# A selective-scan block with two feed-forward layers on one core: the split of a layer norm's last step between GpSimdE and VectorE, two and two tiles or three and one

## The chip, the cores and the metric

One core of a Trainium2 chip. The time is device microseconds (us) of one execution; of several executions the median counts. Engines: TensorE (PE in rows; PEld its weight loads), VectorE (DVE), ScalarE (ACT), GpSimdE (POOL), SyncE (SP), which issues most DMAs.

## What is computed

Two sequences of 2048 tokens of width 256, float32. Every `_layernorm` below has no scale and no offset.

```python
x = x + 0.5 * ffn(_layernorm(x), W1, b1, W2, b2)      # 8 groups of 512 tokens, own weights each
x = x + ssm(_layernorm(x), ...)                        # state-space layer, 512 channels x 16 states
x = x + 0.5 * ffn(_layernorm(x), W1, b1, W2, b2)

def ffn(x): h1 = x @ W1.T + b1 ; return h1 @ W2.T + b2  # linear twice
def step(h, inp):                                       # in ssm, over the tokens
    dt_t, u_t = inp
    h = h * exp(dt_t * A) + dt_t * Bm * u_t             # per channel and state
    return h, sum over states of h * Cm
out = (ys * silu(z)) @ Wo.T + bo + x * Dv.mean()        # z, u, dt from x @ Wi.T + bi
```

## The kernel before, in words

The 4096 tokens go through in four iterations of 1024 (`NIT`, `TOK`). In each there are four blocks of 128 channels, 16 blocks `k` in all, and of each block 16 **scans**: one VectorE instruction (line 1209) runs the recurrence over 1024 tokens for 128 pairs of channel and state, in place in one of 8 buffers of `G` (`NG`). Blocks 0 and 15 are cut in halves of 512 tokens, so there are 288 scans.

Beside each scan there is fixed work: ScalarE makes its factor (`exp`, line 1089) in the same `G` buffer. After four scans TensorE sums over states into `Y` (`red`, line 1376) and so sets free the four buffers that ScalarE fills for the scans 8 places on. Everything else (projections, feed-forward layers, norms, output projection, merging W1 and W2 into one matrix) is cut in chains of small steps.

What sets the order: `schedule` walks the scans and after each lets every waiting chain give out its next step. `PLAN`, `DTS` and `PROJ` say after which scan a chain starts, `rest_for(WAIT)` keeps a step back by some scans. Each engine has the same list and executes its own part strictly in that order; semaphores tie the engines together. So the order is fixed when the kernel is built, whatever the durations are.

A **norm** is the chain `norm(c)`, `c` from 0 to 23, six for each iteration: of 512 tokens, which are four tiles of 128 tokens x 256. Its steps: `sq` on ScalarE (line 910), then `var` (823), `rstd` (832, a power), `sr` (837) and `off` (842) on tiny 128x4 operands, then the normalising itself, `xn = v * rstd + off`, one instruction of 128x256 a tile. Norms 0 to 3 and 23 are `early(c)`: VectorE does nearly all, and nothing is changed in them. Of the other 19 all small steps run on GpSimdE, and the last step is split: `norm` on GpSimdE (line 849) does tiles 2 and 3, `vnorm` on VectorE (line 1186) does tiles 0 and 1, placed among the scans at least six scans behind `norm` where `rest_for(WAIT)` applies. I number these 19 norms in the order of time, norm 1 to norm 19.

Both parts must be done before TensorE transposes the result (`xt`, line 1280); ScalarE copies it out (`xtc`, line 936). GpSimdE's queue also holds `skip` (lines 860 to 863: eight 128x256 tiles in each iteration, in place in `X`) and `msv` (line 869: two 128x256 tiles of a merged weight matrix, for which TensorE's line 1260 waits).

Of the kernel before, what the change touches and what calls it, by code (L numbers as in the profile page):

```python
# [100 lines left out]
def early(c):  # L101

    return c < 4 or c == 23


def made(stage, c):

    return ("v" if early(c) else "") + stage


def normed(c):

    return ("vnorm",) if early(c) else ("norm", "vnorm")
# [513 lines left out]
def build(nc, x, w, wit, wdt, wot, bo, cols, masks, out):  # L627
# [3 lines left out]
    with ctx:  # L631
# [67 lines left out]
        def tiles(pr):  # L699

            return slice(2 * pr[0], 2 * pr[0] + 2) if pr else slice(0, 4)

        def tokens(c):
            it, ph, hf = c // 6, c % 6 // 2, c % 2
            return it, ph, hf, X[:, (2 * it + hf) % NX, :, :], LV[:, c % 6, :, :], XN[:, place[c] % 2, :, :]
# [100 lines left out]
        @block.gpsimd  # L806
        def _(eng):
            e = Engine(eng, count, sems)

            def do(stage, *a):  # L810
                if stage == "calm":
                    eng.memset(ZS[:, 0, 0:512], 0.0).then_inc(sems["calm"])
                elif stage == "ones":
                    eng.memset(ONES[:, :], 1.0).then_inc(sems["ones"])
                elif stage == "half":
                    eng.memset(HIGH[:, :], TOP)
                    eng.memset(ZERO[:, :], 0.0)
                    eng.memset(HALF[:, :], -0.5).then_inc(sems["half"])
                elif stage == "var":
                    c, = a  # L820
                    lv = tokens(c)[4]
                    e.wait_ge("sq", c)
                    eng.tensor_scalar(lv[:, 1, :], lv[:, 1, :], 2.0 ** -24, EPS, ALU.mult, ALU.add).then_inc(sems["var"])  # L823
                elif stage == "rstd":
                    c, *pr = a
                    lv, ts = tokens(c)[4], tiles(pr)
                    e.wait_ge(made("var", c), *a)
                    e.wait_ge("half")
                    if c >= 6:
                        for part in normed(c - 6):  # L830
                            e.wait_ge(part, c - 6)
                    eng.tensor_tensor(lv[:, 3, ts], lv[:, 1, ts], HALF[:, ts], ALU.pow).then_inc(sems["rstd"])  # L832
                elif stage == "sr":
                    c, = a
                    lv = tokens(c)[4]
                    e.wait_ge("rstd", c)
                    eng.tensor_tensor(lv[:, 2, :], lv[:, 0, :], lv[:, 3, :], ALU.mult).then_inc(sems["sr"])
                elif stage == "off":
                    c, = a
                    lv = tokens(c)[4]  # L840
                    e.wait_ge("sr", c)
                    eng.tensor_scalar(lv[:, 4, :], lv[:, 2, :], -1.0 / 256, float(c % 6 // 2 != 1), ALU.mult, ALU.add
                                      ).then_inc(sems["off"])
                elif stage == "norm":
                    c, = a
                    _, _, _, v, lv, xn = tokens(c)
                    e.wait_ge("off", c)
                    for i in (2, 3):
                        ins = eng.tensor_scalar(xn[:, i, :], v[:, i, :], lv[:, 3, i:i + 1], lv[:, 4, i:i + 1],  # L849
                                                ALU.mult, ALU.add)  # L850
                    ins.then_inc(sems["norm"])
                elif stage == "skip":
                    c, i = a
                    _, _, _, v, lv, _ = tokens(c)
                    e.wait_ge("dmu")
                    e.wait_ge(made("sr", c), c)
                    for part in normed(c):
                        e.wait_ge(part, c)
                    if i == 0:
                        eng.tensor_scalar(lv[:, 5, :], lv[:, 3, :], DM[:, 0:1], 1.0, ALU.mult, ALU.add)  # L860
                        eng.tensor_scalar(lv[:, 6, :], lv[:, 2, :], DM[:, 1:2], -1.0, ALU.mult, ALU.mult).then_inc(sems["skips"])
                        eng.wait_ge(sems["skips"], (count.value["skip", a] + 3) // 4)
                    eng.tensor_scalar(v[:, i, :], v[:, i, :], lv[:, 5, i:i + 1], lv[:, 6, i:i + 1],  # L863
                                      ALU.mult, ALU.add).then_inc(sems["skip"])
                elif stage == "msv":
                    g, = a
                    e.wait_ge("mv", g)
                    for i in range(2):
                        ins = eng.tensor_scalar(MS[:, i, 0:256], MS[:, i, 0:256], 1.0, MV[:, i:i + 1], ALU.mult, ALU.add)  # L869
                    ins.then_inc(sems["msv"])  # L870

            schedule(do)
# [222 lines left out]
        def _(eng):  # L1095
            e = Engine(eng, count, sems)

            def do(stage, *a):
# [61 lines left out]
                elif stage == "vvar":  # L1160
                    c, *pr = a
                    lv, ts = tokens(c)[4], tiles(pr)
                    e.wait_ge("sq", *a)
                    eng.tensor_scalar(lv[:, 1, ts], lv[:, 1, ts], 2.0 ** -24, EPS, ALU.mult, ALU.add).then_inc(sems["vvar"])  # L1164
                elif stage == "vsum":
                    c, = a
                    it, _, hf, v, lv, _ = tokens(c)
                    e.wait_ge("x", 2 * it + hf)
                    eng.tensor_reduce(lv[:, 0, :], v, AX.X, ALU.add).then_inc(sems["vsum"])  # L1169
                elif stage == "vsr":  # L1170
                    c, *pr = a
                    lv, ts = tokens(c)[4], tiles(pr)
                    e.wait_ge("rstd", *a)
                    eng.tensor_tensor(lv[:, 2, ts], lv[:, 0, ts], lv[:, 3, ts], ALU.mult).then_inc(sems["vsr"])
                elif stage == "voff":
                    c, *pr = a
                    lv, ts = tokens(c)[4], tiles(pr)
                    e.wait_ge("vsr", *a)
                    eng.tensor_scalar(lv[:, 4, ts], lv[:, 2, ts], -1.0 / 256, float(c % 6 // 2 != 1), ALU.mult, ALU.add
                                      ).then_inc(sems["voff"])  # L1180
                elif stage == "vnorm":
                    c, *pr = a
                    _, _, _, v, lv, xn = tokens(c)
                    e.wait_ge(made("off", c), *a)
                    for i in range(4 if early(c) else 2)[tiles(pr)]:
                        ins = eng.tensor_scalar(xn[:, i, :], v[:, i, :], lv[:, 3, i:i + 1], lv[:, 4, i:i + 1],
                                                ALU.mult, ALU.add)
                    ins.then_inc(sems["vnorm"])
                elif stage == "w":
                    k, p = a  # L1190
                    t0, t1 = span(k, p)
                    for hf in halves(k, p):
                        e.wait_ge("u", k, hf)
                    e.wait_ge("dt", k, p)
                    d = DW[:, 1, t0:t1]
                    eng.tensor_tensor(d, d, DW[:, 0, t0:t1], ALU.mult).then_inc(sems["w"])
                elif stage == "scan":
                    i, = a
                    k, p, m, q = parts(i)
                    t0, t1 = window(k, p)  # L1200
                    idx = states(i)
                    e.wait_ge("repw", k, q, fed(k, p))
                    e.wait_ge("exp", i)
                    goes_on = p > 0 or k // 4 % 2 > 0
                    if goes_on:
                        ko, po = (k, p - 1) if p else scanned(k - 4)
                        e.wait_ge("save", AT[ko, po, 4 * m])
                    g = G[:, i % NG, t0:t1]
                    eng.tensor_tensor_scan(g, g, RV[:, (4 * k + q) % NR, t0:t1], STT[:, idx:idx + 1] if goes_on else 0.0,  # L1209
                                           ALU.mult, ALU.add).then_inc(sems["scan"])  # L1210
                elif stage == "yz":
                    k, p = a
                    t0, t1 = window(k, p)
                    e.wait_ge("red", AT[k, p, 12])
                    for hf in sides(k, p):
                        e.wait_ge("z", k, hf)
                    z = ZS[:, k % NZ, t0:t1]
                    eng.tensor_tensor(z, z, Y[:, t0:t1], ALU.mult).then_inc(sems["yz"])  # L1218
# [239 lines left out]
```

## Time and profile before

| | us |
|---|---|
| median of 3 runs | 768.38 (767.89 to 770.54) |
| the profiled execution | 768.11 |
| its span in the trace | 766.3 |
| VectorE busy | 669.7 (87%) |
| TensorE matmuls busy | 640.7 (84%) |
| ScalarE busy | 603.2 (79%) |
| GpSimdE busy | 301.7 (39%) |

Of 38 `norm` instructions on GpSimdE one takes 2.2 us on average, of 58 on VectorE 0.45 us. A VectorE instruction overlaps the one behind it by 0.08 us in the rows, so its cost in a queue is its duration less that. Scans of 1024 tokens last 2.25 to 2.5 us.

### The profile page before, as it was taken

Reading aid. Unit: us, or ns where it says so; the run is one execution under the profiler, and the core shown is the slowest. Engines: PE = TensorE matmul, PEld = TensorE weight load, DVE = VectorE, ACT = ScalarE, POOL = GpSimd, SP = SyncE. Lnnn points to the kernel's source line nnn. Section 1 sums busy time; section 2 is a strip of 40 time slices with the busy share of each in tenths; the row PEclk is TensorE's granted clock in tenths of the full one; section 3 lists DMA queues with packets and bytes.
Section 4 is the critical chain, followed back from the end, with each engine's and each line's share of the span. In section 5 each row is a group of like instructions: output and inputs, shape, how many; then the busy total and the mean of one; then the engine's idle time right before and its main releaser. Section 6 shows DMA issues by size and latency. Waiting matters only on the chain. (4 is left out here: it accounts for less than half of the span.)

```text
span 766.3 us, 8284 instructions
## 1 busy us (share of the span) xinstructions
PE 640.7 (84%) x2912; PEld 331.8 (43%) x2912; DVE 669.7 (87%) x463; ACT 603.2 (79%) x1066; POOL 301.7 (39%) x189
## 2 busy tenths in 40 slices
PE   7967786889886999979898999967867997874958
PEld 5642333364342466445244574622322654241727
DVE  2436948779999999999999999999999999999791
ACT  2478896779798989998788989898889787946454
POOL 0107020034344598569920767066940060600030
PEclk9997898989997899999999999996988999896979
DMA  8330476350838070421567150705161504205001
GB/s 299 139 137 28 160 219 184 125 178 28 313 117 313 1 246 2 172 103 60 215 198 269 50 198 13 262 1 219 28 216 59 216 31 176 99 28 219 2 0 56
DMA packets 40026, 103.08 MB, mean 135 GB/s; under 512 B 4080, under 2 KB 13040, under 8 KB 39984
## 3 DMA queue, kind: packets, MB, share of 16 engines
q1 hardware_dynamic: 37424, 94.40, 33.7%
q10 hardware_dynamic: 2560, 8.14, 4.5%
q8 instruction: 23, 0.38, 0.2%
q14 instruction: 19, 0.16, 0.1%
HBM read 23.08 MB, written 4.19 MB: 36 GB/s over the span
## 5 line engine op out<-in xcount | busy, mean ns | idle before, releaser
L1089 ACT ACTIVATE G<-RD,COL 128x1024 f32<-128x1024 f32 (+1 forms) x288 | 280.0, 1043 | 62.0 <-PE Y L1376 55.6
L1209 DVE TENSOR_TENSOR_SCAN G<-G,STT,RV 128x1024 f32<-128x1024 f32 (+1 forms) x160 | 312.5, 2015 | 6.4 <-ACT G L1089 6.4
L1209 DVE TENSOR_TENSOR_SCAN G<-G,RV 128x1024 f32<-128x1024 f32 (+1 forms) x128 | 268.9, 2157 | 13.4 <-ACT G L1089 13.4
L1376 PE MATMUL Y<-G,RW 128*32 128x512 f32 x1024 | 143.7, 678 | 62.2 <-DVE G L1209 58.9
L823 POOL TENSOR_SCALAR LV<-LV 128x4 f32<-128x4 f32 x19 | 16.2, 854 | 298.0 <-ACT XN L910 297.7
L1376 PEld LDWEIGHTS Y<-G,RW 128*32 128x32 f32 x1024 | 27.8, 116 | 143.2 <-DVE G L1209 81.5
L849 POOL TENSOR_SCALAR XN<-X,LV 128x256 f32<-128x256 f32 x38 | 83.9, 2212 | 2.0
L1343 PE MATMUL MB<-XI,DIAG 128*64 128x512 f32 x248 | 62.8, 644 | 13.0 <-DMA XI<-XI 11.1
L1302 PE MATMUL MB<-MT,XF 128*128 128x256 f32 x240 | 62.3, 406 | 13.3 <-ACT MT L952 7.6
L832 POOL TENSOR_TENSOR LV<-LV,HALF 128x4 f32<-128x4 f32 (+1 forms) x25 | 45.9, 1837 | 63.5 <-DVE LV L1164 61.9
L1321 PE MATMUL MB<-XT,WI 128*128 128x512 f32 x128 | 64.1, 629 | 3.7 <-ACT XT L936 3.7
L863 POOL TENSOR_SCALAR X<-X,LV 128x256 f32<-128x256 f32 x32 | 63.9, 2007 | 0.8
L1354 PE MATMUL MB<-XT,WI 128*128 128x512 f32 x128 | 59.6, 614 | 3.4 <-ACT XF L936 2.6
L1400 PE MATMUL MB<-WO,ZS 128*128 128x256 f32 x256 | 61.8, 379 | 0.0
L869 POOL TENSOR_SCALAR MS<-MS,MV 128x256 f32<-128x256 f32 x12 | 27.2, 2271 | 85.2 <-DVE MV L1143 85.2
L1302 PEld LDWEIGHTS MB<-MT,XF 128*128 128x128 f32 x240 | 48.3, 203 | 22.8 <-ACT XF L936 9.3
L1400 PEld LDWEIGHTS MB<-WO,ZS 128*128 128x128 f32 x256 | 48.8, 191 | 6.7
L1250 PE MATMUL MB<-W 128*128 128x257 f32 x192 | 47.9, 395 | 2.6 <-DMA W<-in_w 2.5
L910 ACT ACTIVATE XN<-X,LV 128x256 f32<-128x256 f32 x96 | 47.5, 499 | 1.6 <-DVE LV L1169 1.1
L1009 ACT ACTIVATE XI<-MB,COL 64x512 f32<-64x512 f32 x64 | 43.3, 676 | 4.0 <-PE MB L1321 3.5
L1156 DVE SCALAR_TENSOR_TENSOR DW<-MB,COL,DW 128x512 f32<-128x512 f32 x32 | 22.2, 732 | 25.7 <-ACT DW L1067 25.7
L1250 PEld LDWEIGHTS MB<-W 128*128 128x128 f32 x192 | 35.2, 192 | 20.8 <-issue 9.7
(93 smaller groups left out, 774.5 us busy)
## 6 DMA issues: line engine op xcount, KB each, us to landing
RD<-DW SPq DMA_DIRECT2D x60, 512.0 KB, 3.8
RV<-DW SPq DMA_DIRECT2D x60, 512.0 KB, 4.7
W<-in_w SPq DMA_DIRECT2D x48, 256.5 KB, 3.7
XI<-XI ACTq DMA_DIRECT2D x30, 256.5 KB, 5.0
X<-in_x SPq DMA_DIRECT2D x8, 512.0 KB, 5.6
out<-X SPq DMA_DIRECT2D x7, 512.0 KB, 3.2
G<-in_w SPq DMA_DIRECT2D x4, 513.0 KB, 7.8
RV<-in_w SPq DMA_DIRECT2D x4, 513.0 KB, 12.3
```

The costliest lines, as they stand in the source:

```text
L849: ins = eng.tensor_scalar(xn[:, i, :], v[:, i, :], lv[:, 3, i:i + 1], lv[:, 4, i:i + 1], ALU.mult, ALU.add)
L863: eng.tensor_scalar(v[:, i, :], v[:, i, :], lv[:, 5, i:i + 1], lv[:, 6, i:i + 1], ALU.mult, ALU.add).then_inc(sems["skip"])
L910: ins = eng.activation(xn[:, i, :], v[:, i, :], ACT.Square, bias=lv[:, 0, i:i + 1], scale=-256.0, accum_out=lv[:, 1, i:i + 1])
L1089: eng.activation(G[:, i % NG, t0:t1], RD[:, q, t0:t1], ACT.Exp, scale=NAC[:, states(i):states(i) + 1]).then_inc(sems["exp"])
L1209: eng.tensor_tensor_scan(g, g, RV[:, (4 * k + q) % NR, t0:t1], STT[:, idx:idx + 1] if goes_on else 0.0, ALU.mult, ALU.add).then_inc(sems[" ...
L1250: ins = eng.matmul(bank("merge", g, i)[:, 0:257], v[:, 257 + 128 * i:385 + 128 * i], v[:, 0:257], start=(c == 0), stop=(c == 7))
L1302: ins = eng.matmul(o, xf[:, j, 128 * t:128 * t + 128], MT[:, g % NX, j, :], start=False, stop=(i == 1 and j == 1))
L1321: ins = eng.matmul(bank("xim", k, hf), WI[:, j, 128 * ct:128 * ct + 128], XT[:, j, 512 * hf:512 * hf + 512], start=(j == 0), stop=(j == 1))
L1343: ins = eng.matmul(bank("um", k, hf)[64 * g:64 * g + 64, :], DIAG[:, 4 * ct + 2 * g + t, :], XI[:, g, 512 * hf + 2 * t:512 * hf + 2 * t + ...
L1354: ins = eng.matmul(bank("zm", k, hf), WI[:, j, 512 + 128 * ct:640 + 128 * ct], XT[:, j, 512 * hf:512 * hf + 512], start=(j == 0), stop=(j ...
L1376: ins = eng.matmul(Y[32 * q:32 * q + 32, 512 * h:512 * h + 512], RW[:, states(i + o), :], G[:, (i + o) % NG, 512 * h:512 * h + 512], start ...
L1400: ins = eng.matmul(o, ZS[:, (4 * it + ct) % NZ, 128 * (2 * pr + i):128 * (2 * pr + i) + 128], WO[:, ct, :], start=False, stop=(i == 1 and ...
```

## The change

Each of the 19 norms that are not early gives one more tile to GpSimdE: tiles 1, 2 and 3 there, tile 0 on VectorE. Early norms keep all their four on VectorE; norm 23, in two pairs, keeps them too.

```diff
                 elif stage == "norm":
                     e.wait_ge("off", c)
-                    for i in (2, 3):
+                    for i in (1, 2, 3):
                         ins = eng.tensor_scalar(xn[:, i, :], v[:, i, :], lv[:, 3, i:i + 1], lv[:, 4, i:i + 1],
                                                 ALU.mult, ALU.add)
...
                 elif stage == "vnorm":
                     e.wait_ge(made("off", c), *a)
-                    for i in range(4 if early(c) else 2)[tiles(pr)]:
+                    for i in range(4 if early(c) else 1)[tiles(pr)]:
```

No instruction changes its place against the others; TensorE, ScalarE and SyncE have the same lists. On VectorE, from norm 5 to norm 9 (`L1186` are the norms, `L1209` the scans, 280 to 336 us in the trace), a part of the difference:

```order
-L1186 TENSOR_SCALAR XN<-X,LV 128x256 x2
+L1186 TENSOR_SCALAR XN<-X,LV 128x256
 L1209 SCALAR_TENSOR_TENSOR G<-G,STT,RV 128x1024 x6
-L1186 TENSOR_SCALAR XN<-X,LV 128x256 x2
+L1186 TENSOR_SCALAR XN<-X,LV 128x256
 L1209 SCALAR_TENSOR_TENSOR G<-G,STT,RV 128x1024 x4
-L1186 TENSOR_SCALAR XN<-X,LV 128x256 x2
+L1186 TENSOR_SCALAR XN<-X,LV 128x256
```

These are norms 7, 8 and 9: one tile instead of two stands between the scans, at the same places.

On GpSimdE at the same norms, where one norm's steps stand right behind the other's:

```order
-L849 TENSOR_SCALAR XN<-X,LV 128x256 x2
+L849 TENSOR_SCALAR XN<-X,LV 128x256 x3
 L823 TENSOR_SCALAR LV<-LV 128x4
 L832 TENSOR_TENSOR LV<-LV,HALF 128x4
 L837 TENSOR_TENSOR LV<-LV 128x4
 L842 TENSOR_SCALAR LV<-LV 128x4
-L849 TENSOR_SCALAR XN<-X,LV 128x256 x2
+L849 TENSOR_SCALAR XN<-X,LV 128x256 x3
```

The third tile stands ahead of the next norm's four small steps, and so ahead of the `off` for which that norm's VectorE tile waits.

At norm 11 GpSimdE has a merged weight matrix behind the norm (`MS`, line 869), in the changed kernel:

```order
L837 TENSOR_TENSOR LV<-LV 128x4
L842 TENSOR_SCALAR LV<-LV 128x4
L849 TENSOR_SCALAR XN<-X,LV 128x256 x3
L869 TENSOR_SCALAR MS<-MS,MV 128x256 x2
L823 TENSOR_SCALAR LV<-LV 128x4
```

Three tiles instead of two stand ahead of the two of `MS`.

## Rows read from the trace of the kernel before

**Rows 1.** The page, busy us of each engine.
```profile
PE 640.7 (84%) x2912; PEld 331.8 (43%) x2912; DVE 669.7 (87%) x463; ACT 603.2 (79%) x1066; POOL 301.7 (39%) x189
```
**Rows 2.** Stretches: start:end, length, busy us (instructions) by engine, clock, DMA.
```profile
166.00:300.00 134.00, 119.83 (x570) 61.16 (x567) 131.71 (x79) 120.33 (x204) 79.91 (x43) 0.95 0.42 146
300.00:440.00 140.00, 124.78 (x584) 60.82 (x583) 138.38 (x80) 123.08 (x202) 83.53 (x43) 0.98 0.41 144
440.00:582.00 142.00, 117.59 (x562) 57.52 (x562) 140.24 (x81) 123.92 (x217) 79.56 (x43) 0.90 0.39 136
```
**Rows 3.** Waits: engine, tile, line, releaser; total us, times, longest.
```profile
DVE G L1209 <- ACT G L1089: 19.8, 9, 5.5
...
PE MB L1260 <- POOL MS L869: 7.4, 3, 4.3
...
DVE XN L1186 <- POOL LV L842: 0.7, 2, 0.4
```
**Rows 4.** Groups by form: the two lines that the change touches.
```profile
L1186 DVE TENSOR_SCALAR XN<-X,LV 128x256 f32<-128x256 f32 x58 | 23.4, 450 | 0.9 <-POOL LV L842 0.7
...
L849 POOL TENSOR_SCALAR XN<-X,LV 128x256 f32<-128x256 f32 x38 | 83.9, 2212 | 2.0
```
**Rows 5.** Timeline of VectorE: start, us to the last end, line, count.
```profile
296.97 0.72 DVE L1186 TENSOR_SCALAR XN<-X,LV 128x256 f32<-128x256 f32 x2
...
466.83 9.03 DVE L1209 TENSOR_TENSOR_SCAN G<-G,RV 128x1024 f32<-128x1024 f32 x4
...
479.91 21.90 DVE L1209 TENSOR_TENSOR_SCAN G<-G,RV 128x1024 f32<-128x1024 f32 x10
```
**Rows 6.** Timeline of GpSimdE: single norm tiles at three places.
```profile
102.23 0.56 POOL L849 TENSOR_SCALAR XN<-X,LV 128x256 f32<-128x256 f32 x1
...
471.52 4.55 POOL L849 TENSOR_SCALAR XN<-X,LV 128x256 f32<-128x256 f32 x1
...
512.15 2.51 POOL L849 TENSOR_SCALAR XN<-X,LV 128x256 f32<-128x256 f32 x1
```
**Rows 7.** Timeline at norm 5: GpSimdE, then TensorE there and around.
```profile
277.07 5.33 POOL L849 TENSOR_SCALAR XN<-X,LV 128x256 f32<-128x256 f32 x2
282.49 2.04 POOL L823 TENSOR_SCALAR LV<-LV 128x4 f32<-128x4 f32 x1
...
248.57 3.64 PE L1376 MATMUL Y<-G,RW 128*32 128x512 f32 x16 [0.95 <-DVE G L1209]
...
286.32 1.04 PE L1280 MATMUL MB<-COL,XN 128*128 128x128 f32 x8
...
310.21 1.93 PE L1376 MATMUL Y<-G,RW 128*32 128x512 f32 x16 [0.19 <-DVE G L1209]
```
**Rows 8.** Timeline at norm 9 and behind it: GpSimdE, VectorE, ScalarE.
```profile
328.67 2.04 POOL L823 TENSOR_SCALAR LV<-LV 128x4 f32<-128x4 f32 x1
...
335.52 0.91 DVE L1186 TENSOR_SCALAR XN<-X,LV 128x256 f32<-128x256 f32 x2 [0.32 <-POOL LV L842]
...
354.57 4.60 DVE L1209 TENSOR_TENSOR_SCAN G<-G,STT,RV 128x1024 f32<-128x1024 f32 x2 [1.09 <-ACT G L1089]
...
353.38 4.27 ACT L1089 ACTIVATE G<-RD,COL 128x1024 f32<-128x1024 f32 x4
```
**Rows 9.** Timeline at norm 11: the merged weights on GpSimdE, their transpose.
```profile
436.09 4.85 POOL L869 TENSOR_SCALAR MS<-MS,MV 128x256 f32<-128x256 f32 x2
...
443.60 0.60 PE L1260 MATMUL MB<-COL,MS 128*128 128x128 f32 x4
```
**Rows 10.** Timeline at norms 14 and 15: GpSimdE's small steps, VectorE.
```profile
514.75 0.20 POOL L823 TENSOR_SCALAR LV<-LV 128x4 f32<-128x4 f32 x1
515.03 3.10 POOL L832 TENSOR_TENSOR LV<-LV,HALF 128x4 f32<-128x4 f32 x1
...
518.83 0.91 DVE L1186 TENSOR_SCALAR XN<-X,LV 128x256 f32<-128x256 f32 x2 [0.38 <-POOL LV L842]
...
425.37 1.02 POOL L832 TENSOR_TENSOR LV<-LV,HALF 128x4 f32<-128x4 f32 x1
```
**Rows 11.** Timeline at norm 19, the last: GpSimdE and TensorE.
```profile
741.65 3.11 POOL L849 TENSOR_SCALAR XN<-X,LV 128x256 f32<-128x256 f32 x2
...
743.97 1.93 PE L1376 MATMUL Y<-G,RW 128*32 128x512 f32 x8 [2.77 <-DVE G L1209]
```

## The prediction

> **What bounds the kernel now.** I read the page first: VectorE is the busiest engine, 669.7 of 766.3 us, GpSimdE has the most room [rows 1]. A share over the whole span proves little, so the stretches come next. From 166 to 582 us VectorE works 131.71 of 134, 138.38 of 140 and 140.24 of 142 us (the rows overlap by 0.08 us an instruction, so true idle time is a little more); TensorE and ScalarE are at 83 to 90% there [rows 2]. Read alone, this says that a microsecond off VectorE is a microsecond off the kernel. The waits say otherwise: VectorE still waits nine times, 19.8 us in all, for ScalarE's factors [rows 3], and in the saturated part one of these waits is at 354.57 us (1.09 us) [rows 8]. Such a wait pins the time to another engine: what VectorE had saved on the way there it would only wait longer. Last, who waits for GpSimdE: TensorE for the merged weights, 7.4 us in three waits, and VectorE for `off` in two short ones, 0.7 us [rows 3]. GpSimdE has room on average, but some of its results are taken the moment they are ready.
>
> **What is removed.** 19 instructions on VectorE. Two in a row with no neighbour on GpSimdE take 0.72 us [rows 5]; less the overlap, 0.32 each. Their mean is 450 ns [rows 4], so 0.37 with the dearer ones. Gross: 19 x 0.32 = 6.1 us, to 19 x 0.37 = 7.0 us.
>
> **What is added.** 19 instructions on GpSimdE. Where no scan runs one takes 0.56 us; beside scans 2.51 or 4.55 us [rows 6], mean 2.2 [rows 4]. The pattern in the rows: a tile issued inside a scan with another scan behind ends 0.2 us behind the *second* scan's end (4.55 us, at 471.52); one with something short behind the scan ends behind the first (2.51 us, at 512.15). A third tile is issued just where the second ended, most often 0.2 us into a scan, so I take 4.6 us where two scans follow, 2.5 where one does, and 0.56 as the lower end.
>
> The Trainium skill, "SBUF — State Buffer", section "Who interferes with whom", says that a VectorE instruction with two SBUF inputs and a GpSimdE instruction that reads SBUF exclude each other, and that the later one "fully blocks" until the first finishes. The 4.55 us row does not agree: it outlasts the first scan by a whole one.
>
> It also costs VectorE. Ten scans without a big GpSimdE instruction take 21.90 us, 2.18 each; four with one that ends among them take 9.03 instead of 8.80 us [rows 5], so 0.23 us at most for one; other places with several give about 0.1, and the tile that ends beside another instruction may cost nothing. I take 0.13, range 0 to 0.23. Net on VectorE 0.32 - 0.13 = 0.2 us a norm (0.1 to 0.37).
>
> **Which norms' gains reach the end.** Norms 1 and 2 lie ahead of 166 us, where VectorE waits for others. TensorE waits for a scan at 248.57 us and then not again before 310.21 [rows 7]; the wait at 354.57 hangs on ScalarE's exponentials from 353.38 us [rows 8], whose chain leads back over projections on TensorE to that unbroken run. So norms 5 to 9 gain nothing by this count, nor 11 and 12 in the like run of TensorE from 414 to 475 us, nor 18 and 19. Left are norms 3, 4, 10, 13, 14 and 16, and at most norm 17: 6 x 0.2 = **-1.2 us**.
>
> **Where the third tile is late.** Four places.
>
> *Norm 5.* Its two tiles end at 277.07 + 5.33 = 282.40, TensorE takes them at 286.32 [rows 7]: slack 3.9 us. A third tile beside scans adds 4.6: TensorE waits 0.7 us. With one tile gone on VectorE the next scan stands earlier, so the second tile, too, may find two scans instead of one: 2 us more, 2.7. TensorE has no gap before 310, so this passes on. Range 0 to 2.7, I take the middle of 0.7 and 2.7 and round down: **+1.6**.
>
> *Norms 8 and 9.* GpSimdE starts norm 9 at 328.67, right behind norm 8, and VectorE already waits 0.32 us for its `off` at 335.52 [rows 8]. A later start moves VectorE's wait. GpSimdE had 12 us of room ahead of norm 8, but norms 5, 6 and 7 stand back to back and bring 2.5 to 4.6 us each with them. By the steps I get a start of norm 9 some 6 us later, of which most is given back, because once VectorE stands still the four small steps take 0.2 + 1.0 + 0.2 + 0.2 us (1.02 for the power [rows 10]) in place of 8: VectorE waits 2.3 us at norm 9 and 0.3 at norm 8. Against this stand the gains of norms 5 to 9 (1.0), the 1.09 us that it waits at 354.57 anyway, and norm 5's 1.6 by which ScalarE is later there: **0**, range 0 to +2.6.
>
> *Norm 11.* The merged weights end at 436.09 + 4.85 = 440.94, TensorE takes them at 443.60 [rows 9]: slack 2.66. The third tile adds 2.5 to 4.6: 0 to 1.9 us of wait in an unbroken run of TensorE. **+1.0**.
>
> *Norm 15.* The second tile of norm 14 is issued at 512.15 and ends at 514.66 [rows 6]; norm 15's steps start at 514.75 and VectorE waits for them at 518.83, 0.38 us [rows 10]. The third tile (2.6 us) moves the start to 517.3. A tensor_tensor of two SBUF inputs runs to 518.1, then the steps take 0.2 + 1.0 + 0.3 + 0.2: the tile starts at 519.85 instead of 518.83. **+1.0**, range 0 to 2.6. Its own three tiles, two beside scans, end some 7 us later than now, but TensorE then stands idle until about 528.8 us, and so this hides; its cover is gone if they take over 9 us.
>
> At norm 19 the tiles end at 741.65 + 3.11 = 744.76. TensorE is busy on the sums from 743.97 to 745.90 [rows 11]; a third at 0.58 (the neighbour is a VectorE tile, not a scan) ends at 745.3: nothing. The other norms have 5 us of room or more behind them.
>
> **Sum.** -1.2 + 1.6 + 0 + 1.0 + 1.0 = +2.4 us. On the profiled execution, 768.11 us (span 766.3 and 1.8 around it), 770.5; it stood 0.3 us under the median of 768.38, so 770.8 us.
>
> **Rivals.**
>
> *The saving wins.* The pinned stretches are not pinned, since the order lets gains through over ScalarE's slack, and the third tile fits in the rooms. Then 16 norms from the third to the eighteenth give 0.2 each, -3.2 us, less one wait of about 0.4: 765.6. For it: VectorE is at 98% for over 400 us [rows 2]. Against: the wait at 354.57, and that GpSimdE's lateness has to be under 2.66 us at norm 11 and 3.9 at norm 5. It decides where third tiles average below 2.5 us.
>
> *One scan is waited for, not two.* A third tile costs 2.5 us everywhere. Norm 5's slack of 3.9 and norm 11's of 2.66 hold, only norm 15's wait stays: -1.2 + 1.0 = -0.2, so 768.2. For it: the mean of 2.2 us [rows 4]. Against: the 4.55 us row stands exactly where third tiles will.
>
> This is what the skill's rule, named above, would make of it: blocked to the end of the running instruction and no further.
>
> *The backlog passes on.* Norms that stand back to back hand their delay on and nothing gives it back: 2.7 at norm 5, 2.6 at norms 8 and 9 (VectorE behind TensorE's delay, not beside it), 1.9 and 2.6 at norms 11 and 15, less 1.2: +8.6, of which two parts overlap; I take +6.5, 774.9. For it: VectorE waits at `off` of norms 9 and 15 already. Against: the small steps are fast once VectorE stands.
>
> *It does not do what it says:* excluded, since the lists of both engines show one instruction less and one more at each of the 19 places.
>
> **Chances.** Forecast 0.45 (769 to 773.5, half over and half under the bound), one scan 0.20 (0.14 within, 0.06 faster), saving wins 0.15, backlog 0.20. What a measurement can tell from no change is 0.3%, here 2.3 us: under 766.1 or over 770.7. Faster 0.06 + 0.15 = 0.21; same 0.20 + 0.14 = 0.34; slower 0.25 + 0.20 = 0.45. The range takes in the savings case and most of the backlog: 765.4 to 775.5.
>
> **What the profile after will show.** Line 849 x57 at a mean over 2.6 us, GpSimdE busy some 50 us more, line 1186 x39. VectorE's waits for line 842 (0.7 us now) grow to 3 us or more, at norms 8, 9 and 15, and TensorE's waits for line 849, absent now, appear at norm 5. If these waits stay under 1 us the forecast is wrong towards faster; if `L1209 <- L1089` grows by the whole saving, the pinning is right. Scans beside third tiles longer by over 0.3 us each would make it wrong towards slower.

## The result

| | before | after |
|---|---|---|
| median | 768.13 us | 781.61 us (776.49 to 785.23, 4 executions) |
| ratio, 95% interval | | 1.0169 (1.0122 to 1.0216) |
| the profiled execution | 768.11 | 785.23 |
| its span | 766.3 | 783.4 |

The changed kernel is slower by 1.7%, some 13 us. The forecast was 770.8 us with a range up to 775.5: the sign was right, the size far too small. Ratios here and below leave out executions that lie over 1.5% above the fastest of their kernel: two of the ten of n11_only, whose median without them is 771.2 us, and one of the kernel before, at 1583 us.

The page of the kernel after, busy us of each engine, answers [rows 1]:

```profile
PE 651.5 (83%) x2912; PEld 336.6 (43%) x2912; DVE 664.8 (85%) x444; ACT 604.0 (77%) x1066; POOL 322.4 (41%) x208
```

VectorE is 4.9 us lighter, GpSimdE 20.7 us heavier, as the diff says. TensorE, whose instructions are the same, is busy for 10.8 us more. That is the first hint of where to look, and no more than a hint: roomy15 below is 0.5% slower than before and has 648.1 us there.

The groups by form of the kernel after, the two lines of the change ([rows 4]):

```profile
L849 POOL TENSOR_SCALAR XN<-X,LV 128x256 f32<-128x256 f32 x57 | 120.0, 2113 | 2.0
...
L1186 DVE TENSOR_SCALAR XN<-X,LV 128x256 f32<-128x256 f32 x39 | 15.5, 428 | 2.7 <-POOL LV L842 2.4
```

The mean of a GpSimdE tile has not grown (2.11 us, 2.21 before). An average says nothing here; what counts is which tiles are the dear ones. The waits of the kernel after (us in total, times, longest), against [rows 3]:

```profile
DVE G L1209 <- ACT G L1089: 27.1, 11, 5.5
...
PE MB L1280 <- issue: 12.6, 2, 9.9
...
PE MB L1260 <- POOL MS L869: 10.5, 3, 4.2
...
DVE XN L1186 <- POOL LV L842: 2.4, 3, 1.8
```

VectorE waits 7.3 us more for ScalarE's factors, which is more than the 4.9 us that it is less busy. TensorE waits 3.1 us more for the merged weights (3.9 at norm 11, where it did not wait before, and less elsewhere), and 12.6 us in two places ahead of the transposes of `XN` (line 1280). "issue" names no releaser, but the first of them ends 0.1 us behind the end of GpSimdE's third tile; here are both queues at norm 5, timelines of GpSimdE and TensorE of the kernel after (start, us to the last end):

```profile
279.98 9.85 POOL L849 TENSOR_SCALAR XN<-X,LV 128x256 f32<-128x256 f32 x3
...
289.94 1.06 PE L1280 MATMUL MB<-COL,XN 128*128 128x128 f32 x8 [2.71 <-issue]
```

279.98 + 9.85 = 289.83, and TensorE goes on at 289.94.

**Where the time is.** The scans are the same 288 instructions in the same order in every kernel, so the starts of the same few scans, read from VectorE's timeline, cut the span into stretches that can be compared. The stretches run from the last four scans ahead of norm 5's VectorE tiles to the wait at 354.57 us, then to the scan at 425.47, over norm 11 to 477.71, to 507.46, over norms 14 to 16 to 577.82 (times of before), and to the last scan. Two of these starts, the kernel before and then after:

```profile
425.47 2.28 DVE L1209 TENSOR_TENSOR_SCAN G<-G,RV 128x1024 f32<-128x1024 f32 x1
...
477.71 2.28 DVE L1209 TENSOR_TENSOR_SCAN G<-G,RV 128x1024 f32<-128x1024 f32 x1
```

```profile
431.86 2.29 DVE L1209 TENSOR_TENSOR_SCAN G<-G,RV 128x1024 f32<-128x1024 f32 x1
...
489.98 2.28 DVE L1209 TENSOR_TENSOR_SCAN G<-G,RV 128x1024 f32<-128x1024 f32 x1
```

So norm 11's stretch has grown from 52.2 to 58.1 us. The same for all stretches and for the kernels of the experiments below (us, worked out from such starts; in bold where three tiles at a tight norm stand in it):

| kernel | first scan of the cut | norm 5 | between | norm 11 | between | norms 14 to 16 | to the last scan |
|---|---|---|---|---|---|---|---|
| before | 270.15 | 84.4 | 70.9 | 52.2 | 29.8 | 70.4 | 164.8 |
| after | 270.81 | **87.6** | 73.5 | **58.1** | 30.1 | **73.2** | 165.7 |
| tight4 | 266.96 | **92.1** | 74.1 | **58.3** | 29.9 | **72.2** | 164.9 |
| roomy15 | 269.61 | 85.6 | 71.1 | 52.1 | 29.9 | 71.7 | 165.9 |
| n5_only | 268.73 | **92.1** | 74.1 | 52.7 | 29.9 | 70.4 | 164.8 |
| n5_again | 268.33 | **91.1** | 72.2 | 52.5 | 29.9 | 70.4 | 165.5 |
| n11_only | 268.70 | 83.5 | 73.8 | **59.0** | 30.1 | 70.4 | 165.2 |
| n15_only | 270.50 | 83.3 | 73.6 | 52.9 | 29.9 | **70.9** | 165.1 |

The kernel after loses 3.2 us at norm 5, 5.9 at norm 11, 2.8 at norms 14 to 16, and 0.3 to 0.9 us in each of the other parts of the span. The 2.6 us "between" norm 5 and norm 11 are not the change's: n15_only and n11_only have the kernel before's code up to there and show 2.7 and 2.9 too. It is the profiled execution of before that is quick there, as the granted clock shows (stretches 369 to 407 us; busy us of PE, PEld, DVE, ACT, POOL, then clock and DMA), before and after:

```profile
369.00:407.00 38.00, 32.72 (x146) 12.99 (x144) 37.83 (x22) 31.66 (x44) 19.71 (x8) 0.99 0.62 206
```

```profile
369.00:407.00 38.00, 33.95 (x136) 13.83 (x128) 35.11 (x21) 29.35 (x38) 20.84 (x9) 0.91 0.54 185
```

Each kernel has one trace, so an entry of the table is good to about 1 us: over norm 5, too, n11_only and n15_only have the code of before, and they take 83.5 and 83.3 us where before took 84.4. Against them the kernel after loses 4.2 us there, not 3.2. The two spans differ by 17.1 us and the medians by 13.5; the profiled execution of the kernel after is itself 3.6 us above its median.

The scans themselves are not what grew: the durations of all 288 add up to 598.4 us before and 599.9 after, and those beside a third tile are mostly 0.10 to 0.14 us longer.

### The profile page after: what moved, and what is told of

It is laid out like the page before. It is cut to its first block, busy times and chain, and to the rows that moved or that the text cites. A ratio compares the mean times of both kernels' runs of the same rounds, so it can differ in the third digit from the quotient of the medians.

```text
span 783.4 us, 8284 instructions
## 1 busy us (share of the span) xinstructions
PE 651.5 (83%) x2912; PEld 336.6 (43%) x2912; DVE 664.8 (85%) x444; ACT 604.0 (77%) x1066; POOL 322.4 (41%) x208
## 4 chain that ended last, share of the span: by engine, by line
PE 47%; ACT 26%; POOL 8%; DVE 7%; DMA 5%; issue 5%; ACTq 1%; SPq 0%; DVEq 0%; POOLq 0%
ACT G L1089 11%; PE Y L1376 9%; DVE G L1209 6%; PE MB L1400 6%; PE MB L1302 6%; POOL XN L849 5%; PE MB L1250 5%; PE MB L1343 5%; PE MB L1354 5%; DMA XI<-XI 3%; ACT XI L1009 3%; PE MB L1321 3%; PE MB L1294 2%; PE MB L1396 2%; ACT XN L910 2%
## 5 line engine op out<-in xcount | busy, mean ns | idle before, releaser
L1209 DVE TENSOR_TENSOR_SCAN G<-G,STT,RV 128x1024 f32<-128x1024 f32 (+1 forms) x160 | 313.2, 2017 | 11.8 <-ACT G L1089 10.7
L1209 DVE TENSOR_TENSOR_SCAN G<-G,RV 128x1024 f32<-128x1024 f32 (+1 forms) x128 | 269.9, 2165 | 16.6 <-ACT G L1089 16.5
L823 POOL TENSOR_SCALAR LV<-LV 128x4 f32<-128x4 f32 x19 | 19.0, 1000 | 296.4 <-ACT XN L910 296.0
L849 POOL TENSOR_SCALAR XN<-X,LV 128x256 f32<-128x256 f32 x57 | 120.0, 2113 | 2.0
L1343 PE MATMUL MB<-XI,DIAG 128*64 128x512 f32 x248 | 66.3, 674 | 10.4 <-DMA XI<-XI 8.6
L1400 PE MATMUL MB<-WO,ZS 128*128 128x256 f32 x256 | 65.1, 394 | 0.0
L863 POOL TENSOR_SCALAR X<-X,LV 128x256 f32<-128x256 f32 x32 | 56.2, 1766 | 0.8
L1400 PEld LDWEIGHTS MB<-WO,ZS 128*128 128x128 f32 x256 | 51.0, 199 | 7.7
L1250 PE MATMUL MB<-W 128*128 128x257 f32 x192 | 49.6, 406 | 1.9 <-DMA W<-in_w 1.9
L1280 PE MATMUL MB<-COL,XN 128*128 128x128 f32 x184 | 28.4, 305 | 20.7 <-issue 12.6
```

The costliest lines, as they stand in the source:

```text
L1250: ins = eng.matmul(bank("merge", g, i)[:, 0:257], v[:, 257 + 128 * i:385 + 128 * i], v[:, 0:257], start=(c == 0), stop=(c == 7))
L1343: ins = eng.matmul(bank("um", k, hf)[64 * g:64 * g + 64, :], DIAG[:, 4 * ct + 2 * g + t, :], XI[:, g, 512 * hf + 2 * t:512 * hf + 2 * t + ...
L1400: ins = eng.matmul(o, ZS[:, (4 * it + ct) % NZ, 128 * (2 * pr + i):128 * (2 * pr + i) + 128], WO[:, ct, :], start=False, stop=(i == 1 and ...
```

## The experiments

Ratios are to the kernel before, run on the same chip between the others, with 95% intervals. Where a kernel has one line more, line 849 is L850, 1209 is L1210 and so on.

### Which norms carry it: tight4 and roomy15

```diff
+THIRD = (12, 18, 20, 11)
...
-                    for i in (2, 3):
+                    for i in ((1, 2, 3) if c in THIRD else (2, 3)):
...
-                    for i in range(4 if early(c) else 2)[tiles(pr)]:
+                    for i in range(4 if early(c) else 1 if c in THIRD else 2)[tiles(pr)]:
```

These are norms 5, 11, 15 and 16 in the order of the program. roomy15 has the other fifteen numbers in `THIRD`.

> The third tile goes to GpSimdE only at norms 5, 11, 15 and 16, the four behind which TensorE waits 2.7, 3.9, 9.9 and 1.9 us in the changed kernel. Lateness theory: these four carry nearly all of the loss, 10 to 14 us slower than before (778 to 782). Contention theory (every third tile lengthens VectorE's scans): 4 of 19 of the loss, 3 us slower (771). Clock theory (TensorE's clock falls after the waits and this is most of the loss): as the first in time, but with TensorE busy 8 us or more above before.

> The other 15 norms give their third tile to GpSimdE, the four stay at two and two. Lateness theory: no place where TensorE waits for GpSimdE beyond what it did before; 0 to 2 us faster than before (766 to 768). Contention theory: 15 of 19 of the loss, 10 us slower (778).

**tight4** 780.08 us, 1.0169 (1.0126 to 1.0213). **roomy15** 771.28 us, 1.0053 (1.0033 to 1.0073). Four of 19 norms cost as much as the whole change. The two parts make 2.2% together, the change 1.7%; the intervals are too wide to call that a difference, but one cost of roomy15 is not there in the kernel after, as the rows below show. And fifteen norms together, each of which frees VectorE of a tile, gain nothing; they lose half a per cent, which neither expectation had (766 to 768 or 778). One of their losses is the wait that the prediction worked out at norms 8 and 9 (2.3 us). GpSimdE, TensorE and VectorE of roomy15:

```profile
322.49 11.88 POOL L850 TENSOR_SCALAR XN<-X,LV 128x256 f32<-128x256 f32 x3
...
334.42 1.97 PE L1281 MATMUL MB<-COL,XN 128*128 128x128 f32 x8 [3.07 <-POOL XN L850]
...
336.34 0.41 DVE L1187 TENSOR_SCALAR XN<-X,LV 128x256 f32<-128x256 f32 x1 [2.18 <-POOL LV L843]
```

Norm 8's three tiles end at 334.37; only then can GpSimdE make norm 9's `off`, for which VectorE waits 2.18 us. In the kernel after the same wait is 0.32 us, as before the change [rows 8].

### One norm at a time: n5_only, n11_only, n15_only

```diff
+THIRD = (12,)
```

and `(18,)` and `(20,)`, the rest as in tight4.

> The third tile goes to GpSimdE at norm 5 alone. Lateness theory: TensorE waits 2.7 to 4.9 us for norm 5 (it did in the two runs with it), the scans behind are 3 us later from about 312 us on, and the kernel is 2 to 5 us slower than before. If the places add up only with the others, less than 2 us.

> The third tile at norm 11 alone, behind which GpSimdE has two tiles of merged weights. The prediction's step gives a TensorE wait of 0 to 1.9 us at line 1260 and 1 us in all. If the runs so far show the size (waits of 3.9 and 4.1 us there, the scans 6.7 us later from 452 to 480 us): 4 to 7 us slower.

> The third tile at norm 15 alone. Lateness theory: TensorE waits 6 to 9 us for it near 540 us, most of it time in which it stood idle before anyway (4.8 us), 1 to 3 us slower. Prediction's step: 1 us.

**n5_only** 777.61 us, 1.0112 (1.0067 to 1.0158). **n11_only** 772.64, 1.0054 (1.0022 to 1.0086). **n15_only** 770.93, 1.0026 (0.9993 to 1.0058). One moved instruction of 128x256 at norm 5 costs about 1% of the kernel, 9.4 us where I had expected 2 to 5 of that run; norm 11 alone is at the lower end of what was expected, and for norm 15 alone the interval takes in no change. The queues, GpSimdE and TensorE of n5_only:

```profile
277.90 11.97 POOL L850 TENSOR_SCALAR XN<-X,LV 128x256 f32<-128x256 f32 x3
...
289.97 1.94 PE L1281 MATMUL MB<-COL,XN 128*128 128x128 f32 x8 [4.90 <-ACT X L988]
...
293.41 2.63 PE L1401 MATMUL MB<-WO,ZS 128*128 128x256 f32 x8
```

The three tiles end at 289.87, TensorE goes on 0.1 us behind; the releaser that the row names had long been done. Then two things are to be seen. TensorE waits 4.90 us, not the 0.7 to 2.7 of the prediction. And its next instructions are slow: eight transposes take 1.94 us, in [rows 7] 1.04; eight matmuls at line 1401 take 2.63, a little further on and at full clock 1.89. The granted clock of those us (stretch of n5_only, columns as above):

```profile
290.00:295.50 5.50, 5.50 (x19) 4.76 (x20) 5.50 (x4) 4.12 (x15) 5.25 (x4) 0.55 0.00 0
```

Taken by single microseconds the rows say 0.50 from 290 to 294 us, the lower of the two levels (1.2 GHz of 2.4), and 1.00, the upper, from 295 us on. TensorE had stood idle for 4.9 us ahead of it.

At norm 11 the same, GpSimdE and TensorE of n11_only:

```profile
433.04 10.60 POOL L850 TENSOR_SCALAR XN<-X,LV 128x256 f32<-128x256 f32 x3
...
448.62 1.09 PE L1261 MATMUL MB<-COL,MS 128*128 128x128 f32 x4 [3.94 <-POOL MS L870]
...
451.21 3.05 PE L1401 MATMUL MB<-WO,ZS 128*128 128x256 f32 x8
```

n15_only shows what cover is worth:

```profile
521.60 11.83 POOL L850 TENSOR_SCALAR XN<-X,LV 128x256 f32<-128x256 f32 x3
...
533.53 1.94 PE L1281 MATMUL MB<-COL,XN 128*128 128x128 f32 x8 [8.87 <-issue]
```

Here TensorE waits longest of the three, 8.9 us, and the stretch grows by 0.6 us only. Before, it stood idle for 4.78 us of that time ahead of a sum (at 528.77, waiting for a scan), and the 3.9 us by which this sum is still later are nearly all made good behind it.

### Is it the missing VectorE tile or the added GpSimdE tile: saving_only, load_only

saving_only takes tile 1 off VectorE and gives it to nobody (TensorE transposes tile 0 in its place):

```diff
-                    for i in range(4 if early(c) else 2)[tiles(pr)]:
+                    for i in range(4 if early(c) else 1)[tiles(pr)]:
```

load_only leaves VectorE its two and lets GpSimdE do one more, into a scratch tile, ahead of its own two:

```diff
+                    eng.tensor_scalar(SCR[:, :], v[:, 1, :], lv[:, 3, 1:2], lv[:, 4, 1:2],
+                                      ALU.mult, ALU.add)
                     for i in (2, 3):
```

> Only the saving: VectorE normalises one tile of each of the 19 norms, GpSimdE two, and tile 1 is normalised by nobody (TensorE transposes tile 0 in its place). If VectorE is the bound through the scans: 16 x 0.32 = 5 us faster (763). If TensorE and ScalarE pin the pace as the prediction says: 2 us faster (766). If nothing is gained, 768.

> Only the load: GpSimdE does three tiles of each of the 19 norms, the third into a scratch tile that nobody reads, and VectorE keeps its two. Lateness theory: as the changed kernel, less its small saving: 14 to 17 us slower than before (782 to 785). If the loss had to do with the shorter stretch on VectorE (the second tile on GpSimdE falling into two scans instead of one), clearly less than the changed kernel: 775 or under.

**saving_only** 769.76 us, 1.0036 (1.0004 to 1.0068). **load_only** 773.44, 1.0099 (1.0063 to 1.0135). The saving is worth nothing; if anything it costs, although VectorE is 6.6 us less busy. The reason is in GpSimdE's queue at norm 5, where its code is that of before (5.33 us for two tiles in [rows 7]). GpSimdE and VectorE of saving_only:

```profile
272.74 9.50 POOL L849 TENSOR_SCALAR XN<-X,LV 128x256 f32<-128x256 f32 x2
...
274.81 0.39 DVE L1186 TENSOR_SCALAR XN<-X,LV 128x256 f32<-128x256 f32 x1
```

The same two tiles take 4.2 us longer. They are issued at the same place of the same scans (6.92 us behind the scan that starts the cut) in seven traces that can be compared: in the three in which VectorE has two short instructions in a row there (before, n15_only, load_only) they take 2.7 and 2.6 us, in the four in which it has one (saving_only, n5_again, plain_third, narrow_third) 4.9 and 4.6. So VectorE's short instructions are the places at which GpSimdE's tiles get through, and one of them fewer costs each of the two tiles a scan. At norm 15 they take 7.29 us in place of 3.32, and TensorE waits there for 4.6 us.

load_only is the counterpart and fell where its expectation put this case, at 775 us or under. Its three tiles at norm 5 take 9.9 us from 274.14 on, and TensorE hardly waits. GpSimdE (its last two) and TensorE of load_only:

```profile
276.85 7.20 POOL L851 TENSOR_SCALAR XN<-X,LV 128x256 f32<-128x256 f32 x2
...
284.15 1.06 PE L1282 MATMUL MB<-COL,XN 128*128 128x128 f32 x8 [0.59 <-issue]
```

With the same start and one short instruction (n5_again) the three take 14.1 us. So at these two norms about half of what the change does to GpSimdE's tiles comes from what it removes: 4.2 of 8.8 us at norm 5, 4.0 of 8.5 at norm 15, where the three take 11.83.

### What in the third tile is waited for: plain_third, narrow_third

Both against the kernel after. plain_third makes tile 1 from constants, without the two columns of `LV`; narrow_third keeps them and does 4 of 256 columns (TensorE transposes tile 0 in place of tile 1). Both put this tile last:

```diff
-                    for i in (1, 2, 3):
+                    for i in (2, 3):
...
+                    ins = eng.tensor_scalar(xn[:, 1, :], v[:, 1, :], 1.0, 0.0, ALU.mult, ALU.add)
```

```diff
+                    ins = eng.tensor_scalar(xn[:, 1, 0:4], v[:, 1, 0:4], lv[:, 3, 1:2], lv[:, 4, 1:2],
+                                            ALU.mult, ALU.add)
```

> As the changed kernel, but the third tile on GpSimdE comes last and is computed with two constants in place of the two operands from LV (so tile 1 is not normalised). If an instruction with two operands from memory waits for two scans because it must be let in once for these and once for the tile, a third tile now waits for one scan: 2.4 us where it was 4.6, and the kernel is 778 or under. If the second scan is waited for whatever the operands are, it lasts 4.6 as before and the time stays at 780 or more.

> As the changed kernel, but GpSimdE's third tile is only 4 columns wide and comes last (the rest of tile 1 is normalised by nobody, TensorE transposes tile 0 in its place). If the third instruction's time is waiting for VectorE's scans and not work on data, it still lasts 2 to 4.6 us beside scans (about 0.2 alone) and the kernel stays within 3 us of the changed one, 778 to 785. If the size decides, it lasts under 1 us everywhere, and the time is that of the saving alone, 770.

**plain_third** 774.89 us, 1.0095 (1.0064 to 1.0126). **narrow_third** 783.17, 1.0190 (1.0131 to 1.0248). The two third tiles at norm 5, first plain_third, then narrow_third:

```profile
285.11 2.36 POOL L851 TENSOR_SCALAR XN<-X 128x256 f32<-128x256 f32 x1
```

```profile
286.50 4.39 POOL L851 TENSOR_SCALAR XN<-X,LV 128x4 f32<-128x4 f32 x1
```

Both tiles are issued at the same place, 16.40 us behind the scan that starts the cut. A tile of 4 columns takes nearly as long as one of 256 (4.59), and the kernel is as slow as after. A tile of 256 columns without operands from `LV` takes half. So it is no work that is being done in these 4.6 us. With constants the tile is through behind one scan, with two columns of `LV` behind two. The merged weights, with one such operand (line 869), took 4.85 us for two [rows 9], one scan each, though no run here has a norm tile with one.

The Trainium skill, "SBUF — State Buffer", section "Who interferes with whom", has the later instruction blocked until the running one finishes. By that rule plain_third's tile is right (2.36 us, one scan), narrow_third's and those of the kernel after are not (4.39 and 4.59, two scans).

### The other direction: one_three, three_at_tight

one_three gives VectorE three tiles and GpSimdE one in all 19 norms; three_at_tight does so in norms 5, 11 and 15 only.

```diff
-                    for i in (2, 3):
+                    for i in (3,):
...
-                    for i in range(4 if early(c) else 2)[tiles(pr)]:
+                    for i in range(4 if early(c) else 3)[tiles(pr)]:
```

> The other direction: GpSimdE normalises one tile of each of the 19 norms, VectorE three. VectorE-bound theory: 19 x 0.32 = 6 us more on VectorE, 16 of 19 in the stretch where it is busy at 98%: 5 us slower than before (773). Lateness theory: VectorE's longer stretch is partly hidden, and TensorE waits less for GpSimdE: -2 to +3 us (766 to 771).

> Norms 5, 11 and 15 give VectorE three tiles and GpSimdE one, the others are as before. Lateness theory: TensorE never waited for these norms before, so little is to be gained: 0 to 1 us slower by 3 x 0.32 on VectorE, or 1 to 2 us faster if the merged weights behind norm 11 come earlier (766 to 769).

**one_three** 770.14 us, 1.0027 (1.0001 to 1.0054), with 19 instructions more on VectorE (busy 673.7). **three_at_tight** 767.53, 0.9995 (0.9964 to 1.0026). Room at the tight norms beyond what two and two leave is worth nothing: the slacks of 3.9 and 2.66 us cover them. No version beat the kernel before.

### How much of it is the clock: n5_busy, n5_busy5, n5_again

n5_only with matmuls of data at hand put where TensorE waits at norm 5, ten and five in the code, each two on the engine; n5_again is n5_only once more beside n5_busy5:

```diff
+                    if c == 12 and j == 0:
+                        e.wait_ge("wi"); e.wait_ge("wo")
+                        for _ in range(5):
+                            eng.matmul(bank("xt", c, j), WO[:, 0, 0:128], WI[:, 0, 0:512], start=True, stop=True)
```

> As the run with the third tile at norm 5 alone, with ten matmuls of 128x512 put on TensorE ahead of its wait for norm 5 (into the bank that the transposes overwrite), about 4.3 us of work in a wait of 4.9. Clock theory: TensorE's clock stays at its upper level from 285 to 300 us, the step in the scans there falls from 7.8 us to about 5, and the kernel is 2 to 3 us faster than with the idle wait (775). If the wait alone makes the step, it stays at 7 us or more.

> As the last but with five matmuls in the source, which are ten on the engine and 4.3 us of work (ten in the source were 8.7 us and outlasted the wait by 3.6). They fit in the 4.9 us wait for norm 5. Clock theory: TensorE's clock stays at its upper level from 285 to 300 us, the step in the scans from about 285 to 360 us is near 5 us where it was 7.8, and the kernel is 2 to 3 us faster than n5_again. Wait theory: step and time as with the idle wait.

> The third tile at norm 5 alone, once more, on the same chip as the run with the filled wait: 1.1% over before, a half-clock stretch behind the wait.

**n5_busy** 777.49 us, 1.0125 (1.0077 to 1.0173), does not decide between the two, since its 20 matmuls ran for 8.75 us from 282.44 to 291.19, 3.8 us past the end of the tiles at 287.40. **n5_busy5** 773.07, 1.0079 (1.0048 to 1.0110). **n5_again** 775.70, 1.0108 (1.0088 to 1.0128). TensorE of n5_busy5, and its granted clock:

```profile
283.25 4.45 PE L1281 MATMUL MB<-WI,WO 128*128 128x512 f32 x10
288.27 1.09 PE L1286 MATMUL MB<-COL,XN 128*128 128x128 f32 x8 [0.56 <-POOL XN L850]
...
290.06 1.89 PE L1406 MATMUL MB<-WO,ZS 128*128 128x256 f32 x8
```

```profile
286.00:296.00 10.00, 9.44 (x52) 6.13 (x51) 9.89 (x8) 7.27 (x24) 9.56 (x7) 1.00 0.00 2
```

The transposes are late by the same amount, but the clock stays at the upper level. The intervals of the two ratios still touch, so the medians alone, 2.6 us apart, point this way and don't prove it. The trace is sharper. How much later TensorE takes the result, counted from the same scan's start, against how much longer the whole stretch is, both relative to before:

| kernel, place | taken later | stretch longer | rest | TensorE's wait | matmuls behind it longer |
|---|---|---|---|---|---|
| after, norm 5 | 2.95 | 3.16 | 0.2 | 2.71 | 0.0 |
| n5_busy5, norm 5 | 5.02 | 5.00 | 0.0 | 0.56, filled | 0.1 |
| n5_again, norm 5 | 4.93 | 6.73 | 1.8 | 4.76 | 1.5 |
| n5_only, norm 5 | 5.07 | 7.68 | 2.6 | 4.90 | 2.4 |
| after, norm 11 | 4.53 | 5.88 | 1.35 | 3.88 | 1.7 |
| n11_only, norm 11 | 4.52 | 6.75 | 2.2 | 3.94 | 2.4 |
| narrow_third, norm 11 | 4.31 | 3.82 | -0.5 | 3.56 | 0.0 |

(For n5_only: 289.97 - 268.73 = 21.24 against 286.32 - 270.15 = 16.17 in [rows 7] and VectorE's timeline; 92.10 against 84.42.) The lateness passes on in full, within the 1 us to which a stretch is good. The last column does not hang on that: it compares how long TensorE takes from the awaited matmuls to a fixed later one, without a gap. In n5_only the second round of line 1397 (1396 before) starts 5.91 us behind 289.97, before it starts 3.47 us behind 286.32, so 2.4 us are lost; at norm 11 it is the way from line 1260 to the transposes, 4.74 us in the kernel after and 3.03 before. This loss is there in the four rows with idle waits of 3.88 to 4.90 us, and not in those with 2.71 and 3.56 us nor where the wait was filled.

## Why the prediction was wrong

The steps that failed are the sizes in "Where the third tile is late". Norms 5 and 11 stood in the sum with 1.6 + 1.0 = 2.6 us; the profiled execution shows 3.2 + 5.9 = 9.1 there. The mechanism behind them, late tiles ahead of an unbroken run of TensorE, was right. The saving of 1.2 us was not there, and TensorE's clock had no term.

**Right.** That the norms at which TensorE runs without a gap pass a delay on in full; that a third tile beside scans takes 4.6 us, as single tiles of the kernel after show at norm 5:

```profile
279.98 0.69 POOL L849 TENSOR_SCALAR XN<-X,LV 128x256 f32<-128x256 f32 x1
280.67 4.59 POOL L849 TENSOR_SCALAR XN<-X,LV 128x256 f32<-128x256 f32 x1
285.24 4.59 POOL L849 TENSOR_SCALAR XN<-X,LV 128x256 f32<-128x256 f32 x1
```

that with one tile gone on VectorE the second tile, too, meets two scans (before, the two took 2.7 and 2.6), although in four traces the first did as well; that norms 8 and 9 add nothing, though the 2.3 us worked out there do occur where TensorE is not late already (roomy15); that the scans beside third tiles grow by under 0.3 us each; and that nothing happens at norm 19.

**The step "norm 11: +1.0"** is the largest miss: 5.9 us measured. It assumed that the tiles start where they did and added 2.5 to 4.6 us for the third, 0 to 1.9 us of wait. GpSimdE and TensorE of the kernel after, against [rows 9] and the power of 1.02 us in [rows 10]:

```profile
434.23 2.92 POOL L832 TENSOR_TENSOR LV<-LV,HALF 128x4 f32<-128x4 f32 x1
...
438.94 10.60 POOL L849 TENSOR_SCALAR XN<-X,LV 128x256 f32<-128x256 f32 x3
449.53 4.85 POOL L869 TENSOR_SCALAR MS<-MS,MV 128x256 f32<-128x256 f32 x2
...
454.52 0.63 PE L1260 MATMUL MB<-COL,MS 128*128 128x128 f32 x4 [3.88 <-POOL MS L869]
...
455.90 3.53 PE L1400 MATMUL MB<-WO,ZS 128*128 128x256 f32 x8
```

Counted from the scan in front (425.47 and 431.86), the tiles start 7.08 us behind it, 4.57 before: +2.5. Before, `var` and the power stood beside a short VectorE instruction (line 1218) that ends just behind the scan's start, and took 0.20 and 1.02 us; here `var` starts 0.29 us into the scan, and they take 1.99 and 2.92. The tiles take 10.60 instead of 6.06: +4.5. Together 7.0, less the slack of 2.66, is 4.4 late (measured 4.5), and the slow matmuls behind the wait come on top, 1.4 us by the stretch and 1.7 by the rows. The late start is not the third tile's doing: n15_only, with the code of before at norm 11, starts its two tiles 7.07 us behind the scan, too. GpSimdE and TensorE of n15_only:

```profile
434.43 7.98 POOL L850 TENSOR_SCALAR XN<-X,LV 128x256 f32<-128x256 f32 x2
442.39 3.04 POOL L870 TENSOR_SCALAR MS<-MS,MV 128x256 f32<-128x256 f32 x2
...
446.27 0.60 PE L1261 MATMUL MB<-COL,MS 128*128 128x128 f32 x4
```

TensorE takes the result only 0.8 us later there, the stretch being 52.9. Against these rows the third tile adds 2.6 us itself and 1.8 us to the merged weights behind it. The start slips like this in 13 of the 16 traces; the trace of before, from which the slack of 2.66 us was read, is one of the three others. With the late start that slack is 0.8 us. The prediction spent all 2.66 on the third tile.

**The step "norm 5: +1.6"** was mis-sized too: 3.2 us in the kernel after, 6.7 to 7.7 where only norm 5 is changed. The tiles' own +6.6 us (4.6 for the third, 2.0 for the second) is what the step had as its upper end, and less the slack of 3.9 that is its 2.7. I took a value towards the middle although the reason for the upper one stood in the text. Beyond it one more scan is missing: in n5_only the tiles start 9.17 us behind the scan in place of 6.92, in n5_again they start at 6.92 but the first takes 4.92 in place of 2.72. On both ways they end 21.0 to 21.1 us behind the scan, at the end of the same later scan. In the kernel after the first tile slipped through in 0.69 us and they ended 19.0 behind it. That was luck of the execution: tight4, n5_only, n5_busy and n5_busy5 issue this tile 9.16 to 9.17 us behind the scan as well, and there it takes 2.81. Lateness comes in units of a scan here; a range that ends 2.7 us up had no room for one more.

**The clock** had no term. Rows at both levels were in the trace of before, and the waits that the sum gave (1 to 2.7 us) would not have asked for one; the idle waits of 3.9 to 4.9 us at norms 5 and 11 cost 1.5 to 2.4 us more each.

**Norm 15.** The prediction gave 1.0 us to VectorE's wait for `off`, and let the norm's own tiles hide unless they took over 9 us. They took over 9. GpSimdE, TensorE and VectorE of the kernel after:

```profile
532.79 11.83 POOL L849 TENSOR_SCALAR XN<-X,LV 128x256 f32<-128x256 f32 x3
...
544.72 1.94 PE L1280 MATMUL MB<-COL,XN 128*128 128x128 f32 x8 [9.89 <-issue]
...
532.72 0.41 DVE L1186 TENSOR_SCALAR XN<-X,LV 128x256 f32<-128x256 f32 x1 [1.75 <-POOL LV L842]
```

VectorE waits 1.75 us, and the sum behind the transposes comes 5.2 us later than before, counted from the scan at 507.46. The stretch grows by 2.8 us, of which n15_only alone shows 0.6. tight4, which has norms 15 and 16 but not 14, shows 1.8, so some 1.2 us came with norm 16 and some 1.0 with norm 14, each read from one trace. The latter is what the prediction's +1.0 was for, since it is norm 14's third tile that makes norm 15's `off` late; norm 16 it had counted among the norms that gain.

**The saving, -1.2 us,** was not there at all (saving_only, 1.0036). The count of norms whose gain gets through missed that the removed instruction was also a gap for GpSimdE. The price of 0.32 us an instruction holds: the two tiles in [rows 5] did have a neighbour on GpSimdE, the power from 296.87 us, but two at 462.29 us that have none take 0.72 us as well.

**The rivals.** "The saving wins" falls with roomy15 and saving_only. "One scan is waited for" falls with narrow_third; where it holds by construction, plain_third, the kernel still takes 774.9 us and not 768.2, since the removed VectorE tile delays the others (two tiles 9.50 us at norm 5 there too). "The backlog passes on" was the nearest, by the wrong road: at 774.9 us it too lacked the scan more at norm 5 and 11 and the clock, and its part at norms 8 and 9 did not appear. Of the signs named, the waits at line 1280 came; the mean over 2.6 us, 50 us more on GpSimdE and 3 us of VectorE's waits for `off` did not (2.11, 20.7 and 2.4).

**Open** stay 1.6 us near 715 us, which the kernel after, roomy15, saving_only and load_only show and tight4, plain_third and narrow_third do not, the last two changed at the same norms, and why the small steps' phase slips: the rows show that ScalarE's squares end up to 1 us later against the scans, in unchanged code as well.

## What to carry to other kernels

An engine with 60% of its time free is no place for work unless each result that it makes has slack where it is taken: list who takes each one, how long it had lain there, and compare that with the delay rounded up to whole instructions of the neighbour it has to wait out. Short instructions between long ones on one engine can be the openings of another, so count them before removing them. The idle waits of TensorE of 3.9 to 4.9 us cost themselves here and then, in a run without gaps, 1.5 to 2.4 us more for the clock behind them. And a slack read from one trace is that of one execution: compare several before you spend it.

## What the runs showed of the hardware that was not expected

- A GpSimdE `tensor_scalar` beside back-to-back scans lasts for one scan with constants (2.36 us) or one column operand (2.43 each at line 869), and for two with two column operands (4.59), whether it has 256 columns or 4 (4.39). Without scans it takes 0.56 us [rows 6]. What in the instruction has to get through twice is inferred from these forms and was not seen.
- The tiny steps pay as well: the power on 128x4 takes 1.02 us [rows 10] or 2.92, by where it falls.
- Taking an instruction off VectorE made two unchanged GpSimdE instructions slower by 4.2 us (saving_only, norm 5).
- Five matmuls of no use (ten on the engine) in a wait of TensorE kept its clock at the upper level, and the stretch was 1.7 to 2.7 us shorter than without them (89.4 against 91.1 and 92.1).
